# FFN norm statistics from four summed square tiles instead of eight, on eight cores of a Trainium2

## The chip, the cores and the metric

The kernel runs on all 8 cores of one Trainium2 chip, each core with two of the sixteen sequences and no traffic between cores. The metric is the device time of the slowest core in microseconds. The time before is 1403.29 us, the median of 3 runs (1401.22 to 1404.46).

## The reference, cut to what matters

```python
# x: (16, 2048, 1024) f32; weights 1024 x 1024
x = layernorm(x + attn(x))
h = x
for blk in range(3):
    y = qlora_linear(h, q[2*blk], ...)            # dequantised weight + rank-32 term + bias
    y = layernorm(y, gamma[blk], beta[blk])       # over the 1024 features
    y = gelu(y)
    y = qlora_linear(y, q[2*blk+1], ...)
    h = y + h
x = layernorm(x + h)
```

The change is in the inner `layernorm` of the three FFN blocks, in the sum of squares over the 1024 features of a token. The means need no sum: the kernel centres each first weight matrix and its bias over the output features beforehand, so that `y` has mean zero.

## The kernel before, in words

Activations lie transposed: 128 features on the partitions, 512 tokens on the free axis. A sequence has 4 token tiles t of 512, and each of these has 8 feature tiles of 128x512 (`EC = 8`). After attention (which also dequantises the six FFN weights in its background) the FFN runs for each of the core's two sequences g and each block n: `y1(t, n)` for t = 0 to 3, then `y2(t, n, g)` for t = 0 to 3, or in block 2 `y3(t, g)`, which ends with the final norm and the output.

In `y1` each feature tile o is a group: 8 matmuls 128x512 into one PSUM bank, an Identity activation on ScalarE that evacuates the bank to bf16 `FY[t][o]` with the bias (the "evacuation"), and a VectorE multiply `FY*FY` into a bf16 tile `FSQ` (the "square"). A statistic matmul of a matrix of 1/1024 (`ones_b`) with the square adds it into a further bank; after tile 7 this bank holds the variance on all partitions. `finish` (L914) then has ScalarE take Ln and Exp, which gives `FRS`, 1/sqrt(var). VectorE multiplies each `FY` tile by it (L924, the "scaling", bf16 by f32 to bf16), and ScalarE applies Gelu.

The order on every engine's queue is the order in which the Python code emits it. `after_groups(k, fn)` (L195) runs fn at the k-th following `group_end`. A call from inside group o with k = 3 therefore stands behind two further groups on TensorE: the statistic of tile o stands behind group o+2. The Ln of one token tile stands behind group 1 of the next one, so a norm and its Gelus run beside the `y1` of the next token tile.

`pre(0.75, 0.75)` at the start of each group and `post()` at its end place the waiting work: for each group 0.75 scalings (and in block 2, 0.75 of the residual splits of `split_res`, VectorE, bf16 from f32) go onto VectorE's queue ahead of the group's square, and the Gelu of that scaling goes onto ScalarE's queue behind the group's evacuation. The pattern is six scalings and six Gelus in eight groups; the ones left over follow in the next token tile. With t = 0 there is no earlier norm of the block to place.

All instructions are recorded by helpers: L217 is every matmul, L221 every activation, L225 every VectorE tensor-tensor operation, L234 every scalar-tensor-tensor operation. `Queue.put` turns tokens into semaphore waits; a token of the same engine is waited for too (`_waits`, L82).

```python
    FRS = [f32v(a, 512) for a in F_RS]
    FSQ = [b16v(F_SQ + s * 256, 512) for s in range(5)]
```

Of the kernel before, what the change touches and what calls it, by code (L numbers as in the profile page):

```python
# [12 lines left out]
ALU = mybir.AluOpType  # L13
# [5 lines left out]
EC = 8  # L19
# [10 lines left out]
A_P2 = 26624  # L30
# [6 lines left out]
A_MU = 49408  # L37
A_RS = 49920
# [8 lines left out]
F_HB = (0, 6144, A_H + 4096, A_V + 4096)  # L47
F_Y = (A_DO, A_R0, A_H + 6144, A_V + 6144)
F_W = (A_BT, A_WV)
F_RS = (A_P2, A_P2 + 512, A_LORA, A_LORA + 512)  # L50
F_SQ = A_P2 + 1024
F_XR = A_R
F_OUT = (A_R + 2048, A_R + 3072, A_R + 4096, A_R + 5120)

# [72 lines left out]
def build_program():  # L127
# [19 lines left out]
    with ExitStack() as ctx:  # L147
# [47 lines left out]
        def after_groups(n, fn):  # L195
            due.append((groups[0] + n, fn))
            due.sort(key=lambda d: d[0])
# [18 lines left out]
        def mm(out, lhsT, rhs, start, stop, *after, sig=False):  # L216
            return pe.put(lambda e: e.matmul(out, lhsT, rhs, start=start, stop=stop),  # L217
                          *after, sig=sig)
# [5 lines left out]
        def v_tt(out, a, b, op, *after):  # L224
            return dve.put(lambda e: e.tensor_tensor(out, a, b, op), *after)  # L225
# [517 lines left out]
        FY = [[b16v(F_Y[t] + c * 256, 512) for c in range(EC)] for t in range(4)]  # L743
        FW = [[b16v(F_W[s] + c * 512, 1024) for c in range(EC)] for s in range(2)]
        FRS = [f32v(a, 512) for a in F_RS]
        FSQ = [b16v(F_SQ + s * 256, 512) for s in range(5)]
        FXR = [f32v(F_XR + s * 512, 512) for s in range(4)]
        FOUT = [f32v(a, 1024) for a in F_OUT]
        s_fh = [slot() for _ in range(4)]
# [119 lines left out]
        fy_free[0] = (do_free[0], do_free[1], p_att)  # L869
        fy_free[1] = (rg_free[0], p_att)  # L870
        fy_free[2], fy_free[3] = (p_att,), (p_att,)
        frs_free = [(p_att,)] * 4
        fsq_free = [p_att] * 5
        act_att = (act.sem, act.n)
        cnt = {"sq": 0, "rs": 0, "xr": 0, "out": 0, "fo": 0}
        finals = []
# [21 lines left out]
        def y1(t, n):  # L898
# [2 lines left out]
            sb = [None]  # L901
            k_g[t] = [None] * EC

            def stat_mm(o, q, tok):
                if o == 0:
                    sb[0], fr = bank_take()
                else:
                    fr = ()
                p = mm(ps[sb[0]][:], ones_b, FSQ[q], o == 0, o == EC - 1, tok, *fr, sig=True)
                fsq_free[q] = p  # L910
                if o == EC - 1:
                    finish(p)

            def finish(p):  # L914
# [20 lines left out]
            for o in range(EC):  # L935
                pre(0.75, 0.75)
                b, fr = bank_take()
                for c in range(EC):
                    p = mm(ps[b][:], FW[s][c][:, o * 128:(o + 1) * 128], FHB[t][c],
                           c == 0, c == EC - 1, k_fw[w][c], k_hb[t][c],  # L940
                           *(fr if c == 0 else ()), sig=c == EC - 1)
                late = sq_free if (cnt["sq"] == 4) else ()
                ty = a_act(FY[t][o], ps[b][:], AF.Identity, p, k_fb,
                           *(fy_free[t] if o == 0 else ()), *late, bias=fbc(w, o))
                bank_give(b, ty)
                q = cnt["sq"] % 5
                cnt["sq"] += 1
                tq = v_tt(FSQ[q], FY[t][o], FY[t][o], ALU.mult, ty, fsq_free[q])
                post()
                after_groups(3, lambda o=o, q=q, tq=tq: stat_mm(o, q, tq))  # L950
                group_end(8)
            fw_free[s] = (p,)
            fhb_free[t] = (p,)
# [132 lines left out]
        for g in range(NSEQ):  # L1086
            for n in range(NBLK):
                k_res = {t: [None] * EC for t in range(4)} if n == 1 else (k_res if n else {})
                k_lo = {t: [None] * EC for t in range(4)}
                for t in range(4):  # L1090
                    if g == 0 and n == 0:
                        if t == 0:
                            load_h(0, 2)
                            load_h(0, 3)
                        if t in (1, 2):
                            cast_h(t + 1)
                    y1(t, n)
                    if n == 0 and g == 0 and t == 0:

                        while pieces:  # L1100
                            pieces.pop(0)()
                        xr_free = [(rg_free[1],)] * 4
                        fout_free = [(rg_free[2],), (rg_free[2],), (rg_free[3],), (rg_free[3],)]
                    if n == 2:
                        split_res(t)
# [88 lines left out]
```

How the kernel before makes its waits and increments, by code:

```python
    def emit(self, e, last):  # L108
        for todo, fn, sem, by in self.items:
            for s, v in todo:
                e.wait_ge(s, v)
            inst = fn(e)
            if sem is not None:
                inst.then_inc(sem, by)
        for s, v in last:
            e.wait_ge(s, v)
```

## Time and profile before

| what | value |
|---|---|
| median of 3 runs | 1403.29 us |
| the profiled execution, its own time | 1395.1 us |
| its span on the slowest core (core 2) | 1393.5 us |
| spans of the other cores | 1381.3 to 1393.4 us |
| mean granted TensorE clock, by core | 0.975 to 0.981 |

The span runs from the first to the last instruction of the profiled core. The own time is 1.6 us longer, and the median of the unprofiled runs is 8.2 us above it. The FFN takes the part of the span from about 618 us on. In the views, PE is TensorE, DVE is VectorE, ACT is ScalarE, POOL is GpSimd; an "idle before" is the engine's own idle time ahead of an instruction, with what ended it.

### The profile page before, as it was taken

Reading aid. Unit: us, or ns where it says so; the run is one execution under the profiler, and the core shown is the slowest. Engines: PE = TensorE matmul, PEld = TensorE weight load, DVE = VectorE, ACT = ScalarE, POOL = GpSimd, SP = SyncE. Lnnn points to the kernel's source line nnn. Section 1 sums busy time; section 2 is a strip of 40 time slices with the busy share of each in tenths; the row PEclk is TensorE's granted clock in tenths of the full one; section 3 lists DMA queues with packets and bytes.
Section 4 is the critical chain, followed back from the end, with each engine's and each line's share of the span. In section 5 each row is a group of like instructions: output and inputs, shape, how many; then the busy total and the mean of one; then the engine's idle time right before and its main releaser. Section 6 shows DMA issues by size and latency. Waiting matters only on the chain.

```text
span 1393.5 us, 21058 instructions; the slowest of 8 cores (1381.3 to 1393.5 us)
## 1 busy us (share of the span) xinstructions
PE 1300.7 (93%) x6611; PEld 611.1 (44%) x6740; DVE 704.3 (51%) x1487; ACT 746.1 (54%) x1100; POOL 356.1 (26%) x284
## 2 busy tenths in 40 slices
PE   5997999898899999999999999999899999999994
PEld 2444444443344444444444444455444444444552
DVE  1133556543344456446553483677435534736774
ACT  0153226663223276536855884776578558748641
POOL 5022333565543225332000075001100000840010
PEclk9998999999999999999999999999999999999997
DMA  9956546796856345692101055025801010640032
GB/s 136 208 187 208 178 142 165 216 254 234 295 146 212 114 152 186 216 364 87 61 1 61 1 198 165 0 98 206 287 16 61 1 61 20 207 137 1 31 121 91
DMA packets 71371, 192.61 MB, mean 138 GB/s; under 512 B 6032, under 2 KB 16864, under 8 KB 68192
## 3 DMA queue, kind: packets, MB, share of 16 engines
q1 hardware_dynamic: 48352, 133.45, 29.1%
q0 software_dynamic: 22912, 57.81, 15.2%
q8 instruction: 57, 0.93, 0.3%
q14 instruction: 50, 0.41, 0.1%
HBM read 158.85 MB, written 46.15 MB: 147 GB/s over the span
## 4 chain that ended last, share of the span: by engine, by line
PE 72%; DMA 10%; DVE 6%; issue 4%; ACT 4%; POOL 2%; SPq 1%; DVEq 0%; ACTq 0%; POOLq 0%
PE ps L217 72%; ACT POOLT L221 4%; DMA POOLT<-qw_t 3%; DMA POOLT<-xt 2%; DMA x1s<-POOLT 2%; DVE POOLT L225 2%; DVE SM L1032 1%; POOL POOLT L105 1%; DVE SM L234 1%; DMA POOLT<-bv_h 1%; SPq L105 1%; DMA POOLT<-sc_t 1%; DMA POOLT<-lb_h 1%; POOL POOLT L684 1%; DVEq L111 0%
## 5 line engine op out<-in xcount | busy, mean ns | idle before, releaser
L217 PE MATMUL ps<-POOLT 128*128 128x512 bf16 (+3 forms) x5476 | 1225.2, 375 | 37.1 <-DMA POOLT<-wq 11.5
L217 PEld LDWEIGHTS ps<-POOLT 128*128 128x128 bf16 x5600 | 532.9, 98 | 664.5 <-issue 91.7
L221 ACT ACTIVATE POOLT<-ps,SM 128x512 bf16<-128x512 f32 (+4 forms) x396 | 262.2, 682 | 249.3 <-PE ps L217 152.2
L225 DVE TENSOR_TENSOR POOLT<-POOLT 128x512 bf16<-128x512 bf16 (+1 forms) x448 | 256.4, 608 | 209.5 <-ACT POOLT L221 187.0
L221 ACT ACTIVATE POOLT<-POOLT 128x512 bf16<-128x512 f32 (+4 forms) x234 | 175.3, 762 | 225.1 <-DMA POOLT<-qw_t 108.1
L225 DVE TENSOR_TENSOR POOLT<-ps,POOLT 128x512 bf16<-128x512 f32 (+1 forms) x186 | 124.2, 688 | 151.9 <-PE ps L217 126.9
L990 POOL TENSOR_TENSOR POOLT<-POOLT 128x512 f32<-128x512 f32 x64 | 89.6, 1424 | 371.1 <-DMA POOLT<-x1s 361.9
L411 POOL TENSOR_TENSOR POOLT<-POOLT 128x1024 f32<-128x1024 f32 x48 | 112.7, 2348 | 263.1 <-DMA POOLT<-sc_t 169.6
L221 ACT ACTIVATE POOLT<-POOLT,CF 128x512 bf16<-128x512 bf16 x192 | 154.3, 808 | 27.5 <-DVE POOLT L225 26.5
L221 ACT ACTIVATE POOLT<-POOLT,SM 128x512 bf16<-128x512 f32 (+2 forms) x120 | 109.8, 917 | 83.3 <-DVE SM L228 47.8
L234 DVE SCALAR_TENSOR_TENSOR POOLT<-ps,SM,POOLT 128x512 f32<-128x512 f32 x128 | 96.1, 750 | 80.8 <-PE ps L217 80.3
L217 PE MATMUL ps<-POOLT,CB 128*128 128x512 bf16 (+2 forms) x331 | 96.8, 383 | 24.5 <-ACT POOLT L221 13.4
L684 POOL TENSOR_TENSOR POOLT<-POOLT 128x1024 f32<-128x1024 f32 x32 | 75.0, 2362 | 54.7 <-ACT POOLT L221 53.5
L221 ACT ACT_TABLE_LOAD x48 | 61.6, 1283 | 34.8 <-PE ps L217 30.7
L105 POOL DMA_DIRECT2D out<-POOLT x28 | 15.0, 535 | 252.0 <-ACT POOLT L221 252.0
L600 DVE TENSOR_REDUCE SM<-ps 128x1 f32<-128x512 f32 (+3 forms) x80 | 48.9, 611 | 39.7 <-PE ps L217 36.4
L217 PEld LDWEIGHTS ps<-POOLT,CB 128*128 128x128 bf16 (+2 forms) x336 | 25.6, 96 | 66.0 <-issue 45.8
L228 DVE TENSOR_SCALAR POOLT<-ps,SM 128x512 bf16<-128x512 f32 (+1 forms) x36 | 26.9, 755 | 45.8 <-PE ps L217 45.0
L1032 DVE BATCH_NORM_STATS2 SM<-ps 128x6 f32<-128x512 f32 x64 | 43.4, 692 | 10.9 <-PE ps L217 9.0
L217 PEld LDWEIGHTS ps<-CB,POOLT 128*128 128x128 bf16 x512 | 34.4, 99 | 15.4 <-issue 0.6
L217 PE MATMUL ps<-CB,POOLT 128*128 128x128 bf16 x512 | 39.5, 221 | 0.0
L105 POOL DMA_DIRECT2D weffs<-POOLT x48 | 28.6, 597 | 41.8 <-ACT POOLT L221 33.4
(53 smaller groups left out, 250.7 us busy)
## 6 DMA issues: line engine op xcount, KB each, us to landing
POOLT<-qw_t SPq DMA_DIRECT2D x48, 512.0 KB, 4.0
POOLT<-sc_t SPq DMA_DIRECT2D x48, 512.0 KB, 5.5
POOLT<-weffs SPq DMA_DIRECT2D x24, 1024.0 KB, 7.8
POOLT<-xt SPq DMA_DIRECT2D x16, 1024.0 KB, 10.5
x1s<-POOLT POOLq DMA_DIRECT2D x16, 1024.0 KB, 9.2
POOLT<-x1s SPq DMA_DIRECT2D x8, 2048.0 KB, 11.8
POOLT<-x1s SPq DMA_DIRECT2D x64, 256.0 KB, 3.1
out<-POOLT POOLq DMA_DIRECT2D x28, 512.0 KB, 3.8
```

Of the source, the lines that this page charges most:

```text
L105: self.items.append((todo, lambda e: e.dma_start(out=out, in_=in_), slot.sem, 16))
L217: return pe.put(lambda e: e.matmul(out, lhsT, rhs, start=start, stop=stop), *after, sig=sig)
L221: return act.put(lambda e: e.activation(out, in_, func, bias=bias, scale=scale, accum_out=acc), *after)
L225: return dve.put(lambda e: e.tensor_tensor(out, a, b, op), *after)
L228: return dve.put(lambda e: e.tensor_scalar(out, a, s1, s2, op0, op1), *after)
L234: return dve.put(lambda e: e.scalar_tensor_tensor(out, a, s, b, op0, op1, accum_out=acc, reverse1=rev), *after)
L411: dq_ab[s] = pool.put(lambda e: e.tensor_tensor(q, q, f32v(a + 1024, 1024), ALU.mult), t, dq_ld[s][1])
L600: t = dve.put(lambda e, b=b, lo=lo, n=n: e.tensor_reduce(col(ro + n), ps[b][:, lo:512], AX.X, ALU.max, negate=True), p)
L684: ta = pool.put(lambda e: e.tensor_tensor(r3, r3, rb, ALU.mult), t, *k_r)
L990: tr = pool.put(lambda e, h=h, q=q: e.tensor_tensor(h, h, FXR[q], ALU.add), kx, hb[o], th)
L1032: tb.append(dve.put(lambda e, b=b, k2=k2, fo=fo: e.bn_stats(sm[:, fo + 6 * k2:fo + 6 * k2 + 6], ps[b][:]), p, *fin_free[i]))
```

## The change

Each pair of feature tiles now gives one bf16 tile to the statistic: both squares are written in f32 into two work tiles `FTMP`, a third VectorE operation adds them and rounds to bf16, and one statistic matmul takes the sum. A norm has four statistic matmuls in the place of eight. The statistic of a pair is put off by three `group_end` calls from inside its odd group, so it stands behind two further groups. There are six `FSQ` tiles for five, in other places, and three of the four `FRS` tiles move to memory that attention used; the first norm's wait `late` goes, and the tiles' new first waits (for attention's last readers) are set after the first `y1`. No work moves on TensorE but the statistics, and none on ScalarE, GpSimd's or SyncE's queues.

```diff
-F_RS = (A_P2, A_P2 + 512, A_LORA, A_LORA + 512)
-F_SQ = A_P2 + 1024
+F_RS = (A_P2, A_MU, A_RS, A_SQ)
+F_TMP = (A_P2 + 512, A_P2 + 1024)
+F_SQ = tuple(A_P2 + 1536 + 256 * i for i in range(3)) + tuple(A_LORA + 256 * i for i in range(3))
...
-            def stat_mm(o, q, tok):
-                if o == 0:
+            def stat_mm(j, q, tok):
+
+                if j == 0:
                     sb[0], fr = bank_take()
...
-                p = mm(ps[sb[0]][:], ones_b, FSQ[q], o == 0, o == EC - 1, tok, *fr, sig=True)
+                p = mm(ps[sb[0]][:], ones_b, FSQ[q], j == 0, j == 3, tok, *fr, sig=True)
                 fsq_free[q] = p
-                if o == EC - 1:
+                if j == 3:
                     finish(p)
...
-                late = sq_free if (cnt["sq"] == 4) else ()
                 ty = a_act(FY[t][o], ps[b][:], AF.Identity, p, k_fb,
-                           *(fy_free[t] if o == 0 else ()), *late, bias=fbc(w, o))
+                           *(fy_free[t] if o == 0 else ()), bias=fbc(w, o))
                 bank_give(b, ty)
-                q = cnt["sq"] % 5
-                cnt["sq"] += 1
-                tq = v_tt(FSQ[q], FY[t][o], FY[t][o], ALU.mult, ty, fsq_free[q])
+                t2 = v_tt(FTMP[o % 2], FY[t][o], FY[t][o], ALU.mult, ty, ftmp_free[0])
+                if o % 2:
+                    q = cnt["sq"] % NFSQ
+                    cnt["sq"] += 1
+                    tq = v_tt(FSQ[q], FTMP[0], FTMP[1], ALU.add, t2, fsq_free[q])
+                    ftmp_free[0] = tq
+                    after_groups(3, lambda j=o // 2, q=q, tq=tq: stat_mm(j, q, tq))
                 post()
-                after_groups(3, lambda o=o, q=q, tq=tq: stat_mm(o, q, tq))
                 group_end(8)
...
+                        frs_free[1:] = [(*rs_free, *mr_free, *sq_free)] * 3
```

VectorE's queue in `y1` of token tile 2, block 1, of the first sequence. The names are all `POOLT`, the one large memory tile; s3 is ScalarE's semaphore, s1 TensorE's, s2 VectorE's own. Before, from a scaling (no wait) on: the squares of tiles 2 and 3 (one row, x2), a scaling, the square of tile 4, a scaling, the square of tile 5, a scaling, the squares of tiles 6 and 7.

```order
L225 TENSOR_TENSOR POOLT<-POOLT 128x512
L225 TENSOR_TENSOR POOLT<-POOLT 128x512 [waits s3,s1] x2
L225 TENSOR_TENSOR POOLT<-POOLT 128x512
L225 TENSOR_TENSOR POOLT<-POOLT 128x512 [waits s3,s1]
L225 TENSOR_TENSOR POOLT<-POOLT 128x512
L225 TENSOR_TENSOR POOLT<-POOLT 128x512 [waits s3,s1]
L225 TENSOR_TENSOR POOLT<-POOLT 128x512
L225 TENSOR_TENSOR POOLT<-POOLT 128x512 [waits s3,s1] x2
```

The same stretch of the changed kernel, from the square of tile 2 on (the numbers of the lines are one higher): square 2, square 3, their sum (waits s2), a scaling, square 4, a scaling, square 5, sum, a scaling, square 6, square 7, sum.

```order
L226 TENSOR_TENSOR POOLT<-POOLT 128x512 [waits s3,s2]
L226 TENSOR_TENSOR POOLT<-POOLT 128x512 [waits s3]
L226 TENSOR_TENSOR POOLT<-POOLT 128x512 [waits s2,s1]
L226 TENSOR_TENSOR POOLT<-POOLT 128x512
L226 TENSOR_TENSOR POOLT<-POOLT 128x512 [waits s3,s2]
L226 TENSOR_TENSOR POOLT<-POOLT 128x512
L226 TENSOR_TENSOR POOLT<-POOLT 128x512 [waits s3]
L226 TENSOR_TENSOR POOLT<-POOLT 128x512 [waits s2,s1]
L226 TENSOR_TENSOR POOLT<-POOLT 128x512
L226 TENSOR_TENSOR POOLT<-POOLT 128x512 [waits s3,s2]
L226 TENSOR_TENSOR POOLT<-POOLT 128x512 [waits s3]
L226 TENSOR_TENSOR POOLT<-POOLT 128x512 [waits s2,s1]
```

A scaling that stood directly behind the square of an odd tile now stands behind the sum as well, and the sum waits for VectorE's own semaphore.

TensorE's queue at the same place. Before, from the last group ahead of a statistic on: the statistic (`POOLT,CB`, CB holding `ones_b`) stands behind every group of 8 matmuls.

```order
L217 MATMUL ps5<-POOLT 128x512 x7
L217 MATMUL ps0<-POOLT,CB 128x512 [waits s2]
L217 MATMUL ps7<-POOLT 128x512 [waits s3]
L217 MATMUL ps7<-POOLT 128x512 x7
L217 MATMUL ps0<-POOLT,CB 128x512 [waits s2]
L217 MATMUL ps3<-POOLT 128x512 [waits s3]
L217 MATMUL ps3<-POOLT 128x512 x7
L217 MATMUL ps4<-POOLT,CB 128x512 [waits s2,s3]
```

In the changed kernel a statistic stands behind every second group.

```order
L218 MATMUL ps0<-POOLT,CB 128x512 [waits s2]
L218 MATMUL ps3<-POOLT 128x512 [waits s3]
L218 MATMUL ps3<-POOLT 128x512 x7
L218 MATMUL ps1<-POOLT 128x512 [waits s3]
L218 MATMUL ps1<-POOLT 128x512 x7
L218 MATMUL ps4<-POOLT,CB 128x512 [waits s2,s3]
```

The statistic of tiles 2 and 3 comes at the same group as the statistic of tile 3 before, behind group 5; that of the last pair behind group 1 of the next token tile, as before.

## Rows read from the trace of the kernel before

**Rows 1.** The page, busy time of each engine and share of the span

```profile
span 1393.5 us, 21058 instructions; the slowest of 8 cores (1381.3 to 1393.5 us)
...
PE 1300.7 (93%) x6611; PEld 611.1 (44%) x6740; DVE 704.3 (51%) x1487; ACT 746.1 (54%) x1100; POOL 356.1 (26%) x284
```

**Rows 2.** Groups by shape: busy us, mean ns | idle before, releasers

```profile
L225 DVE TENSOR_TENSOR POOLT<-ps,POOLT 128x512 f32<-128x512 f32 x64 | 43.1, 689 | 69.3 <-PE ps L217 59.7 <-DMA POOLT<-xt 9.4
...
L225 DVE TENSOR_TENSOR POOLT<-POOLT 128x512 bf16<-128x512 f32 x64 | 43.8, 685 | 0.0
...
L225 DVE TENSOR_TENSOR SM<-SM 128x2 f32<-128x2 f32 x45 | 7.3, 162 | 5.0 <-DVE SM L234 0.5
...
L217 PE MATMUL ps<-POOLT,CB 128*128 128x512 bf16 x203 | 75.9, 381 | 13.9 <-DVE POOLT L225 10.0 <-ACT POOLT L221 3.7
```

**Rows 3.** Window 1150 to 1200 us: PE, PEld, DVE, ACT, POOL busy; clock; DMA

```profile
1150.00:1200.00 50.00, 48.89 (x224) 22.09 (x227) 29.19 (x49) 43.53 (x60) 10.24 (x7) 1.00 0.27 89
```

**Rows 4.** Timeline of TensorE, statistic matmuls: start, us, what, idle before

```profile
1150.13 1.89 PE L217 MATMUL ps<-POOLT 128*128 128x512 bf16 x8
1151.86 0.38 PE L217 MATMUL ps<-POOLT,CB 128*128 128x512 bf16 x1
...
1160.24 0.38 PE L217 MATMUL ps<-POOLT,CB 128*128 128x512 bf16 x1 [0.45 <-DVE POOLT L225]
...
1176.39 0.38 PE L217 MATMUL ps<-POOLT,CB 128*128 128x512 bf16 x1 [0.45 <-DVE POOLT L225]
```

**Rows 5.** Timeline of ScalarE over the norm between token tiles 1 and 2

```profile
1152.12 0.69 ACT L221 ACTIVATE POOLT<-ps,SM 128x512 bf16<-128x512 f32 x1 [0.56 <-PE ps L217]
1152.70 0.80 ACT L221 ACTIVATE POOLT<-POOLT,CF 128x512 bf16<-128x512 bf16 x1
1153.52 1.28 ACT L221 ACT_TABLE_LOAD   x1
1154.82 0.69 ACT L221 ACTIVATE POOLT<-ps,SM 128x512 f32<-128x512 f32 x1
1155.59 0.63 ACT L221 ACTIVATE POOLT<-POOLT 128x512 f32<-128x512 f32 x1
1156.13 0.67 ACT L221 ACTIVATE POOLT<-ps,SM 128x512 bf16<-128x512 f32 x1
1156.82 1.28 ACT L221 ACT_TABLE_LOAD   x1
1158.11 0.81 ACT L221 ACTIVATE POOLT<-POOLT,CF 128x512 bf16<-128x512 bf16 x1
1158.83 1.24 ACT L221 ACTIVATE POOLT<-ps,SM 128x512 bf16<-128x512 f32 x2
1160.79 0.81 ACT L221 ACTIVATE POOLT<-POOLT,CF 128x512 bf16<-128x512 bf16 x1 [0.72 <-DVE POOLT L225]
1161.51 0.67 ACT L221 ACTIVATE POOLT<-ps,SM 128x512 bf16<-128x512 f32 x1
```

**Rows 6.** Timeline of VectorE: square of tile 3, the scaling behind it

```profile
1159.67 0.42 DVE L225 TENSOR_TENSOR POOLT<-POOLT 128x512 bf16<-128x512 bf16 x1 [2.27 <-ACT POOLT L221]
...
1160.01 0.69 DVE L225 TENSOR_TENSOR POOLT<-POOLT 128x512 bf16<-128x512 bf16 x1
```

**Rows 7.** TensorE idle in block 2, and the clock in two windows behind idle time

```profile
957.74 0.59 PE L217 MATMUL ps<-POOLT 128*128 128x512 bf16 x2 [2.47 <-ACT POOLT L221]
...
1002.39 0.38 PE L217 MATMUL ps<-POOLT,CB 128*128 128x512 bf16 x1 [3.74 <-ACT POOLT L221]
...
1336.73 1.02 PE L217 MATMUL ps<-POOLT 128*128 128x512 bf16 x4 [2.23 <-ACT POOLT L221]
...
1000.00:1008.00 8.00, 5.55 (x18) 2.31 (x20) 1.70 (x4) 4.37 (x7) 1.06 (x2) 0.79 0.93 362
...
1337.00:1340.00 3.00, 2.89 (x16) 1.70 (x16) 2.90 (x6) 3.00 (x6) 1.06 (x2) 0.68 0.37 150
```

**Rows 8.** Timeline of VectorE at the FFN's start, GpSimd multiplying beside it

```profile
630.39 4.79 DVE L225 TENSOR_TENSOR POOLT<-POOLT 128x512 bf16<-128x512 bf16 x1 [0.69 <-ACT POOLT L221]
```

More of the change, by code:

```diff
@@ L745, in build_program @@
         FRS = [f32v(a, 512) for a in F_RS]
-        FSQ = [b16v(F_SQ + s * 256, 512) for s in range(5)]
+        FSQ = [b16v(a, 512) for a in F_SQ]
+        FTMP = [f32v(a, 512) for a in F_TMP]
+        NFSQ = len(FSQ)
         FXR = [f32v(F_XR + s * 512, 512) for s in range(4)]
@@ L871, in build_program @@
         fy_free[2], fy_free[3] = (p_att,), (p_att,)
-        frs_free = [(p_att,)] * 4
-        fsq_free = [p_att] * 5
+        frs_free = [(p_att,), None, None, None]
+        fsq_free = [p_att] * NFSQ
+        ftmp_free = [p_att]
         act_att = (act.sem, act.n)
```

## The prediction

> **What bounds the kernel now.** The page comes first: TensorE is busy for 93% of the span, VectorE and ScalarE for about half [rows 1]. By the page alone a matmul less is time less, and VectorE has room. The window of 50 us inside one FFN block then shows that the mean hides something: TensorE 48.89 of 50, but ScalarE 43.53 [rows 3]. So I read the three engines' timelines around one norm.
>
> TensorE [rows 4]. The eight matmuls of a group take 1151.86 − 1150.13 = 1.73 us, 0.216 each; with its statistic a group takes 1.94. The same statistic, that of tile 3, starts at 1160.24 and 1176.39 in two following token tiles: a period of 16.15 us, where 72 matmuls make 15.54. The missing 0.6 is one wait for VectorE at this statistic. The row of all statistic matmuls [rows 2] has 10.0 us idle for VectorE's sake; token tiles 2 and 3 of the six `y1` stages, 12 norms, have this wait of 0.45.
>
> ScalarE [rows 5] tells why. From the last statistic of the norm (1151.86, call it 0): evacuation of group 1 at 0.26, a Gelu, a table load, Ln, Exp, evacuation 2 only at 4.27, a second table load, a Gelu, evacuation 3 at 6.97. The square of tile 3 starts at 1159.67 [rows 6], 7.81 on this scale, and the statistic at 8.38, where TensorE was ready at 4 x 1.94 = 7.77. So at one place of a norm ScalarE, then VectorE, are the last to be waited for.
>
> **What the change removes.** 96 of 192 statistic matmuls at 0.216: 20.7 us if nothing waits. In the 12 norms that wait, it counts only through what ends last there; the other half, 48, lies in token tiles 0 and 1 and the start of `y2`, where no wait stands: 48 x 0.216 = **−10.4 us**.
>
> **What it adds.** On VectorE 96 sums, and 192 squares with f32 results. A sum reads f32: every tensor-tensor row with an f32 operand has 685 to 689 ns [rows 2], and the scaling, with one f32 input, 0.69 [rows 6]. The square of today, all bf16, takes 0.42 [rows 6]. A bf16-to-f32 square does not occur: it lies between 0.42 and 0.69. I take 0.69, since one f32 operand is enough for it in every row. The Trainium skill (VectorE: DVE Perf Modes, "What auto-detection actually checks") lets two elements a cycle through only where every tensor is 16-bit; by that rule the change loses time, with the fast square it would come out even (below).
>
> The sum waits for VectorE's own semaphore. The small VectorE operations that wait so have 5.0 us idle before 45 of them, 0.11 each [rows 2]. Bounds 0 (with the overlap of 0.09 kept, as square and scaling start 0.34 apart for 0.42 of length [rows 6]) and 0.25; I take 0.11. The skill's same page ("The DRAIN you can't avoid") says a semaphore between two VectorE operations costs nothing extra. By that a link of the chain below shrinks to 3.55 and the total to about 1408; the row has 0.11, and I follow the row.
>
> **Where it lies.** On the new queue a scaling stands behind each odd tile's square and the sum; its Gelu stands on ScalarE ahead of the next evacuation. That closes a chain which TensorE isn't part of. One link: evacuation 3 to square 3, 0.84 (1158.83 to 1159.67 [rows 5, 6]); square and semaphore 0.69 + 0.11; sum, start to start with the scaling behind it, 0.60 (0.69 less the overlap); scaling to Gelu 0.78 (1160.01 to 1160.79 [rows 5, 6]); Gelu to evacuation 5, 0.72 (1160.79 to 1161.51 [rows 5]). Together **3.74 us** for two groups. In the same way from evacuation 5 to 7 and from 7 to 1 of the next token tile. From evacuation 1 to evacuation 3 over both table loads it is 1158.83 − 1152.12 = 6.71 [rows 5], ScalarE's own work, unchanged. A round is 3 x 3.74 + 6.71 = **17.93 us**. TensorE needs 68 matmuls, 14.7 us, and waits for the rest, some 3 us, at the statistic of tiles 2 and 3. Before, the link was 1161.51 − 1158.83 = 2.68 [rows 5], the round 14.75, and TensorE's 16.15 ended last. So each of 12 norms costs 17.93 − 16.15 = 1.78 more: **+21.4 us**.
>
> In block 2 the residual splits share VectorE: for a pair 0.80 + 0.60 for the squares, 0.60 for the sum, 1.5 scalings and 1.5 splits at 0.60 each, 3.80 in all, against TensorE's 17 matmuls, 3.67. In token tile 1 of both passes, where TensorE was the bound, that is 4 x 0.13 each, **+1.0 us**.
>
> The other edits have one answer together, nothing: the places of the tiles, the dropped `late`, and the new first waits, on attention's last readers, which ended long before the second norm. At the FFN's start VectorE operations of 4.79 us stand beside GpSimd's multiplies [rows 8]; four more operations there may cost or move 1 or 2 us; I take 0.
>
> Sum: −10.4 + 21.4 + 1.0 = **+12.0 us**. The profiled execution's span of 1393.5 becomes 1405.5, its own time of 1395.1 becomes 1407.1. The median shown is 8.2 above that execution, so the forecast is 1403.3 + 12.0 = **1415.3 us**. A measurement of this kernel tells about 0.2%, 2.8 us, from no change.
>
> **The clock.** TensorE's idle of 3 us is new. Idle of 2.47 us left the clock at its high level, 2.4 GHz; idle of 2.23 and of 3.74 did not: the granted clock was 0.68 over the 3 us from 1337 and 0.79 over the 8 us from 1000, 1.2 GHz for part of each [rows 7]. The latter is 0.21 x 8 = 1.7 us of matmul time lost. In the new round TensorE has slack of 1.1 between its groups and the chain (statistic at 2.5 behind evacuation 3, then 17 matmuls and 0.26 to evacuation 7: 6.4, against the chain's 7.5), so a fall costs 0.6, or 7 us if all 12 norms have one. That is the top of the forecast's own range, 1408 to 1423. The skill (TensorE: Matmul & The Clock Gate, "What's actually happening") has activity release the throttle and idleness bring it back; no run yet shows which of these waits would.
>
> **The rivals.**
> - *The square stays at 0.42.* Link 3.47, round 17.12: 12 x 0.97 = +11.6, less 10.4: 1404.5 us, no change. For it: nothing but that no row has this operation. Against: all f32 rows.
> - *The chain doesn't close*, since ScalarE makes up its lag between evacuations 3 and 1. Then only the pair's own path is late: evacuation 3 at 6.97 + 0.84 + 0.80 + 0.69 + 0.15 = 9.45, then four groups and two statistics, 7.34: a round of 16.79. 12 x 0.64 − 10.4 = −2.7: 1400.6 us, just at the bound of faster. It decides if the link falls below the 3.67 us that TensorE takes for a pair; mine is above by 0.07 only, but TensorE's start is late too, so it would have to fall a good deal. With 0.42 squares as well it is −5.9, 1397.4.
> - *VectorE's work is hidden, as the page's 51% suggests.* The waits stay at 0.6 and all 96 matmuls count: −20.7, 1382.6 us. This needs the pair's sum ready at 7.34, while evacuation 3 alone starts at 6.97. I see no way.
> - *That the change doesn't do what it says*: the order shows it does.
>
> **Chances.** Forecast 0.66 (with the clock's share); fast square 0.10; open chain 0.17, on both sides of the 0.2% bound; all hidden 0.04; the rest, a size wrong upwards past 1424, 0.03. Faster 0.16, same 0.14, slower 0.70. Range 1400 to 1424 us: from the open chain to the forecast with every clock fall. The likeliest case alone has 1408 to 1423.
>
> **What would show it.** Right: 96 statistic matmuls fewer; two VectorE groups at about 0.69 where the 0.42 squares were; waits of about 3 us on VectorE at the statistic of tiles 2 and 3 in token tiles 2 and 3 of all six stages, 17.9 us apart; ScalarE's Gelus waiting for VectorE after each odd tile. Wrong: waits of 2 us or less there, rounds near 16.8, squares of 0.42, or token tiles 0 and 1 of blocks 0 and 1 longer than 14.7 us. Only the clock would be off if the rounds are longer than 17.9 with a granted clock under 1.00.

## The result and the profile after

The changed kernel takes **1437.8 us** (median of 4 runs, the fastest 1434.9) against 1402.3 before (median of 4); the ratio is 1.0242, 95% interval 1.0222 to 1.0263. So it is slower by 34 us by the ratio, where 12 were forecast and 1424 was the top of the range. A later measurement of the same kernel (e0) gave 1.0253 (1.0201 to 1.0305). Times are medians over all executions, while ratios leave out those in which the cores of one die had a lower granted clock and took some per cent longer.

The page of the changed kernel, the lines that answer to [rows 1]:

```profile
span 1436.7 us, 21083 instructions; the slowest of 8 cores (1415.3 to 1436.7 us)
...
PE 1314.8 (92%) x6644; PEld 605.3 (42%) x6644; DVE 818.9 (57%) x1583; ACT 745.1 (52%) x1100; POOL 355.0 (25%) x284
```

VectorE has 115 us more work and still only 57% of the span. TensorE is busy for 14 us more with 96 matmuls fewer (weight loads x6644 for x6740; some matmul records are missing on the page of before). The groups by shape of core 0, which answer to [rows 2]: line, engine, operation, shapes, count, busy us, mean ns, idle before and its releasers.

```profile
L226 DVE TENSOR_TENSOR POOLT<-POOLT 128x512 bf16<-128x512 bf16 x192 | 139.9, 729 | 0.0
L226 DVE TENSOR_TENSOR POOLT<-POOLT 128x512 f32<-128x512 bf16 x192 | 136.9, 715 | 124.1 <-ACT POOLT L222 123.7
L226 DVE TENSOR_TENSOR POOLT<-POOLT 128x512 bf16<-128x512 f32 x160 | 114.9, 720 | 13.5 <-DVE POOLT L226 8.2 <-PE ps L218 0.2
...
L218 PE MATMUL ps<-POOLT,CB 128*128 128x512 bf16 x110 | 40.9, 383 | 48.8 <-DVE POOLT L226 48.2 <-issue 0.3
```

The second row is the squares, f32 out of bf16; singly they take 0.69 us, and a few that were held up longer raise the mean to 0.715. The third holds the 96 sums and 64 residual splits; 8.2 us of idle there are the sums' waits for VectorE's own semaphore. The last row is the statistic matmuls: they wait for VectorE for 48.2 us, where it was 10.0.

The chain of the forecast can be read off directly. ScalarE on core 0, second sequence, block 1, in the round of token tile 2:

```profile
1180.20 1.24 ACT L222 ACTIVATE POOLT<-ps,SM 128x512 bf16<-128x512 f32 x2
1183.22 0.81 ACT L222 ACTIVATE POOLT<-POOLT,CF 128x512 bf16<-128x512 bf16 x1 [1.78 <-DVE POOLT L226]
1183.94 0.67 ACT L222 ACTIVATE POOLT<-ps,SM 128x512 bf16<-128x512 f32 x1
...
1188.28 0.69 ACT L222 ACTIVATE POOLT<-ps,SM 128x512 bf16<-128x512 f32 x1 [0.51 <-PE ps L218]
...
1198.75 0.67 ACT L222 ACTIVATE POOLT<-ps,SM 128x512 bf16<-128x512 f32 x1
```

VectorE at the same time (square of tile 3, then the sum with three operations behind it, the first of them the scaling):

```profile
1180.97 0.69 DVE L226 TENSOR_TENSOR POOLT<-POOLT 128x512 f32<-128x512 bf16 x1 [1.94 <-ACT POOLT L222]
1181.83 2.50 DVE L226 TENSOR_TENSOR POOLT<-POOLT 128x512 bf16<-128x512 f32 x4 [0.17 <-DVE POOLT L226]
```

Evacuation 3 starts at 1180.20, its square at 1180.97, the sum at 1181.83, the Gelu at 1183.22, evacuation 5 at 1183.94: 3.74 us, the forecast's link to the hundredth. That it is so exact is luck in part: evacuation to square took 0.77 for the 0.84 forecast, square to sum 0.86 for 0.80, and the two misses cancel. TensorE's waits at the statistics of this block:

```profile
1168.49 0.38 PE L218 MATMUL ps<-POOLT,CB 128*128 128x512 bf16 x1 [0.38 <-DVE POOLT L226]
1182.67 0.38 PE L218 MATMUL ps<-POOLT,CB 128*128 128x512 bf16 x1 [2.77 <-DVE POOLT L226]
1201.22 0.38 PE L218 MATMUL ps<-POOLT,CB 128*128 128x512 bf16 x1 [2.03 <-DVE POOLT L226]
```

The window behind the middle one: its length, the busy time (and instructions) of PE, PEld, DVE, ACT and POOL, the granted clock and the DMA's share and rate:

```profile
1182.00:1188.00 6.00, 5.33 (x17) 2.15 (x18) 5.01 (x8) 3.59 (x5) 0.00 (x0) 0.72 0.00 0
```

From 1182.67 to 1201.22 are 18.55 us, not 17.93. The clock stood at 0.72 over 6 us: 0.28 x 6 = 1.7 us of matmul time gone. Evacuation 7 came at 1188.28 for TensorE's sake, 0.60 behind the chain (1183.94 + 3.74 = 1187.68). This is the forecast's "a fall costs 0.6", and it happened.

The FFN's start holds the largest single wait. TensorE, then VectorE, then GpSimd in the timeline of core 7:

```profile
638.89 0.59 PE L218 MATMUL ps<-POOLT,CB 128*128 128x512 bf16 x1 [8.56 <-DVE POOLT L226]
...
627.34 13.60 DVE L226 TENSOR_TENSOR POOLT<-POOLT 128x512 f32<-128x512 bf16 x6
...
627.31 5.08 POOL L685 TENSOR_TENSOR POOLT<-POOLT 128x1024 f32<-128x1024 f32 x2 [12.81 <-ACT POOLT L222]
632.93 0.59 POOL L106 DMA_DIRECT2D x1s<-POOLT  x1 [0.54 <-POOL POOLT L685]
633.54 4.64 POOL L685 TENSOR_TENSOR POOLT<-POOLT 128x1024 f32<-128x1024 f32 x2
```

Six VectorE operations, worth 4 us, lie over 13.6 us. Three of them run beside GpSimd's four multiplies; seen singly they are two squares and their sum:

```profile
627.34 2.85 DVE L226 TENSOR_TENSOR POOLT<-POOLT 128x512 f32<-128x512 bf16 x1
630.12 2.82 DVE L226 TENSOR_TENSOR POOLT<-POOLT 128x512 f32<-128x512 bf16 x1
633.04 5.70 DVE L226 TENSOR_TENSOR POOLT<-POOLT 128x512 bf16<-128x512 f32 x1
```

The sum ends at 638.74, and the statistic that waits for it starts at 638.89. The other three operations come behind the last multiply and take 0.69 or less each. Before, the longest wait at this place was 1.77 us (core 2).

**A measure for the experiments.** Runs differ by some us, also in attention's part. So below stands "the FFN": from the start of VectorE's first 128x2048 cast to the end of the span, as the median of the eight cores. Within a kernel the cores agree here to 1 or 2 us. It is 778.7 us before and 811.3 for the changed kernel in e0, +32.6; the two cores of the changed kernel's first run that had no spells of a clock of 0.81 (see e0) have 810.5 and 811.1. So it is compared across measurements too, e0 being the reference. A "round" is from one norm's Ln to the next; a "tail" from the last Ln of a block's `y1` over its `y2` or `y3` to the next block's first Ln. In blocks 0 and 1 before (past the first block's start): rounds of 16.24, 16.15, 16.35 and a tail of 69.9. A round so measured is that of ScalarE's Lns: the round of token tile 1 in the changed kernel is 16.99 by the Lns (1159.19 to 1176.18 on core 0) and 15.30 by TensorE's last statistics (1156.93 to 1172.23).

### The profile page after: what moved, and what is told of

It reads as the page before. It is cut to its first block, busy times and chain, and to the rows that moved or that the text cites. A ratio compares the mean times of both kernels' runs of the same rounds, so it can differ in the third digit from the quotient of the medians.

```text
span 1436.7 us, 21083 instructions; the slowest of 8 cores (1415.3 to 1436.7 us)
## 1 busy us (share of the span) xinstructions
PE 1314.8 (92%) x6644; PEld 605.3 (42%) x6644; DVE 818.9 (57%) x1583; ACT 745.1 (52%) x1100; POOL 355.0 (25%) x284
## 4 chain that ended last, share of the span: by engine, by line
PE 56%; DVE 11%; DMA 10%; issue 9%; ACT 9%; POOL 2%; SPq 1%; DVEq 1%; ACTq 0%; POOLq 0%
PE ps L218 56%; ACT POOLT L222 7%; DVE POOLT L226 7%; DMA POOLT<-qw_t 4%; DMA x1s<-POOLT 3%; DMA POOLT<-xt 2%; ACT L222 2%; DVE SM L1039 1%; POOL POOLT L106 1%; DVE SM L235 1%; DMA POOLT<-bv_h 1%; SPq L106 1%; DVEq L112 1%; POOL POOLT L685 0%; DMA POOLT<-sc_t 0%
## 5 line engine op out<-in xcount | busy, mean ns | idle before, releaser
L218 PE MATMUL ps<-POOLT 128*128 128x512 bf16 (+2 forms) x5600 | 1242.7, 380 | 26.7 <-ACT POOLT L222 9.2
L226 DVE TENSOR_TENSOR POOLT<-POOLT 128x512 f32<-128x512 bf16 (+2 forms) x544 | 373.2, 721 | 137.7 <-ACT POOLT L222 123.8
L218 PE MATMUL ps<-POOLT,CB 128*128 128x512 bf16 (+2 forms) x240 | 63.7, 387 | 64.1 <-DVE POOLT L226 50.1
L218 PEld LDWEIGHTS ps<-POOLT,CB 128*128 128x128 bf16 (+2 forms) x240 | 16.1, 95 | 104.8 <-issue 98.6
L1039 DVE BATCH_NORM_STATS2 SM<-ps 128x6 f32<-128x512 f32 x64 | 43.2, 689 | 8.0 <-PE ps L218 6.1
L235 DVE SCALAR_TENSOR_TENSOR POOLT<-POOLT,ps 128x512 f32<-128x512 f32 x48 | 30.9, 681 | 14.6 <-POOL POOLT L412 12.3
```

The source lines that it names most:

```text
L235: return dve.put(lambda e: e.scalar_tensor_tensor(out, a, s, b, op0, op1, accum_out=acc, reverse1=rev), *after)
L1039: tb.append(dve.put(lambda e, b=b, k2=k2, fo=fo: e.bn_stats(sm[:, fo + 6 * k2:fo + 6 * k2 + 6], ps[b][:]), p, *fin_free[i]))
```

## The experiments

Theories at the outset: the **chain** (as in the forecast, with too little allowed for the clock and the start) and, as rival, **VectorE's amount of work**, with the order of no account. Diffs are against the changed kernel unless another is named. Ratios are to the kernel before on the same chip.

**e1, the statistic one group later.**

```diff
-                    after_groups(3, lambda j=o // 2, q=q, tq=tq: stat_mm(j, q, tq))
+                    after_groups(4, lambda j=o // 2, q=q, tq=tq: stat_mm(j, q, tq))
```

> The changed kernel, each pair's statistic one group later (three groups behind the pair's odd tile instead of two). Chain theory (the round evacuation, square, sum, scaling, Gelu, next evacuation, with Ln and Exp at its end, and TensorE waiting for the sum of tiles 2 and 3): the wait of 2.8 us at that statistic falls under 1.5 in token tiles 2 and 3, their rounds come down from 17.9 to 15.4 to 17, and the time to 1410 to 1422 us. Rival, VectorE's amount of work is the bound: the rounds stay at 17.9 and the time within 5 us of 1437.8.

Measured: 1417.9 us, ratio 1.0171 (1.0149 to 1.0193), the FFN 798.7, rounds of 18.0, 17.05, 17.4, just above the 15.4 to 17 worked out. The amount of work is the same and 12.6 us are gone, so VectorE's work alone isn't the bound in blocks 0 and 1. In block 2 the rounds grew, to 19.2, 18.8, 19.3, and the whole block took 147.0 us for e0's 146.3: there it didn't help.

**e2, the sum behind the next scaling.** The sum of a pair isn't issued in its group, but in the next `pre`, behind the scaling.

```diff
+            while sum_q:
+                sum_q.pop(0)()
             credit[1] = min(credit[1] + res_rate, 1.75)
...
-                    tq = v_tt(FSQ[q], FTMP[0], FTMP[1], ALU.add, t2, fsq_free[q])
-                    ftmp_free[0] = tq
+                    def pair_sum(q=q, t2=t2):
+                        ftmp_free[0] = v_tt(FSQ[q], FTMP[0], FTMP[1], ALU.add, t2, fsq_free[q])
+                        k_sum[q] = ftmp_free[0]
+                    sum_q.append(pair_sum)
...
```

> The changed kernel with the sum of a pair put behind the next group's scaling on VectorE, so that a scaling is never behind a sum. Same operations, same statistic places. Chain theory: the link is 0.6 to 0.8 us shorter, the pair's own path 0.6 longer; rounds about 17.2 instead of 17.9, the time about 5 to 8 us less, 1430 to 1433. Rival, VectorE's amount of work: no change, 1437.8.

Measured: 1421.3 us, ratio 1.0201 (1.0171 to 1.0230), the FFN 802.8, 8.5 less. Rounds 16.3, 17.13, 17.5. The second round was worked out as 17.2. The order counts.

The same run shows what the sum's own wait costs. Square, scaling and sum of core 0 in one row, the sum third:

```profile
791.34 1.90 DVE L226 TENSOR_TENSOR POOLT<-POOLT 128x512 f32<-128x512 bf16 x3 [1.94 <-ACT POOLT L222]
```

Three operations of 0.69 in 1.90 us, each 0.60 behind the one ahead. The sum still waits for VectorE's semaphore, but one operation stands between it and the square that sets it, and nothing is lost. Directly behind the square, as in the change, it starts 0.79 or 0.86 after it.

**e3, both**, e1's place and e2's order; the matmul takes the token of a sum that is issued later.

```diff
-                    after_groups(3, lambda j=o // 2, q=q, tq=tq: stat_mm(j, q, tq))
...
+                    sum_q.append(pair_sum)
+                    after_groups(4, lambda j=o // 2, q=q: stat_mm(j, q, k_sum[q]))
```

> Both: the sum behind the next scaling, and the statistic one group later. Chain theory: nothing closes; rounds 14.7 to 15.3 in blocks 0 and 1, no wait over 0.6 us at a statistic in token tiles 2 and 3 there, hence no fall of the clock there either; time 1395 to 1405 (the FFN's start still costs 7 to 10). Rival, VectorE's amount of work: rounds 17.9, over 1430.

Measured: 1418.0 us, ratio 1.0173 (1.0151 to 1.0195). This ratio says little: in the profiled run cores 0 and 1 had their clock at 0.81 for 161 us, an FFN of 803 to 805, and set the time. The two other executions that the ratio is taken over have such a pair too, cores 2 and 3 or 4 and 5, with a mean clock of 0.951 to 0.953 and some 20 us longer; the slowest of the six other cores took 1391.2 to 1394.6 us in the three. In the profiled run the FFN of the six others is 777 to 783, as before the change, with rounds of 16.0, 15.8, 16.6 and tails of 67.4 in blocks 0 and 1. These rounds were worked out as 14.7 to 15.3; they missed that by a microsecond. Rounds of 17.4 to 18.9 in block 2 and the start, 31.4 to 34.1 for 24.6, took back what blocks 0 and 1 gave.

**e4, the very first token tile as before** (bf16 squares, eight statistics); all others with pairs.

```diff
+            old = first_y1[0]
...
+                if old:
...
+                    tq = v_tt(FSQ[q], FY[t][o], FY[t][o], ALU.mult, ty, fsq_free[q])
+                    after_groups(3, lambda j=o, q=q, tq=tq: stat_mm(j, q, tq))
...
```

> The changed kernel, with the very first token tile of the FFN as before (bf16 squares, eight statistic matmuls), where GpSimd's multiplies run beside it. Theory, a VectorE operation with two SBUF tensors is held until GpSimd's multiply ends, and the changed kernel has six such operations ahead of its first waiting statistic instead of fewer: the wait of 8.6 us falls to 2 to 4 and the time to 1428 to 1432. Rival, the longer start comes from attention's end or from the moved tiles: the wait stays over 7 us and the time within 3 us of 1437.8.

Measured: 1422.3 us, ratio 1.0197 (1.0179 to 1.0216), the FFN 803.3, 8.0 less. From the first cast to the first Ln it is 24.6 us on six cores (25.9 and 26.0 on two), to the tenth what it was before; the changed kernel has 31.7 to 34.4.

**e11, attention's last four multiplies on VectorE.**

```diff
+                    if (seq, ic) == (1, 3):
+                        for c in (2 * i, 2 * i + 1):
+                            rc = RG[g][:, c * 512:(c + 1) * 512]
+                            ta = v_tt(rc, rc, RS, ALU.mult, t, *k_r)
+                    else:
...
```

> The changed kernel with attention's last four multiplies of 128x1024 on VectorE (as eight of 128x512 in f32, some 5 us of work) instead of GpSimd, nothing else. Theory, VectorE operations with two SBUF tensors are held until GpSimd's running multiply ends: VectorE has more to do, yet the wait at the first statistics falls from 8.6 to under 5 us, no VectorE tensor-tensor operation there takes more than 0.7 us, and the stretch from the FFN's first cast to the first Ln falls from 31.7 to 25-29 us. Rival, only VectorE's amount of work counts there: the wait and the stretch get longer.

Measured: one run, 1420.6 us, beside 1397.7 before; the FFN 802.0, 9.3 less, and 21.5 us to the first Ln. VectorE and TensorE on core 6:

```profile
627.24 7.17 DVE L226 TENSOR_TENSOR POOLT<-POOLT 128x512 f32<-128x512 bf16 x11
634.79 3.90 DVE L226 TENSOR_TENSOR POOLT<-POOLT 128x512 f32<-128x512 bf16 x6 [0.37 <-ACT POOLT L222]
...
643.22 0.38 PE L218 MATMUL ps<-POOLT,CB 128*128 128x512 bf16 x1 [1.97 <-DVE POOLT L226]
```

Seventeen operations in 11 us, where six took 13.6 beside GpSimd. With more work on VectorE the time to the first Ln is shorter than before the change (24.6); at the second Ln the two are level, 43.2 us from the first cast and 43.0 before, where e0 has 51.1. VectorE was held by GpSimd's running multiplies; the rival falls.

**e0, the changed kernel again**, with no edit, beside variants.

> The changed kernel itself once more, beside the variants. If the rounds' length (chain, start of the FFN, falls of the clock to half) is all, its ratio to the kernel before is 1.023 to 1.025 here too, and the FFN of a core without stretches at 13/16 of the clock takes 810 us against 778. If stretches at 13/16 made a good part of the first measurement, the ratio is 1.021 or less on a chip that shows none.

Measured: 1429.0 us, ratio 1.0253 (1.0201 to 1.0305), the FFN 809.7 to 811.5 on all cores, none at 0.81 of the clock. In the first measurement six of eight cores had such spells in the FFN, as core 2 here (the clock of this window is 0.83):

```profile
835.00:845.00 10.00, 10.00 (x41) 4.18 (x40) 8.72 (x10) 8.11 (x13) 10.00 (x7) 0.83 0.66 168
```

The spells come in pairs of neighbouring cores, at the same times in both of a pair. Their FFN took 816 to 823 us, that of the two cores without them 810.5 and 811.1. They are no part of the 34 us: in e0's profiled execution there are none, and the ratio is the same. One other of e0's executions (1441.9 us) has a mean clock of 0.949 and 0.952 on cores 6 and 7; without it the ratio of the means is 1.023.

**e5, bf16 work tiles**, so that square and sum are bf16 throughout.

```diff
-        FTMP = [f32v(a, 512) for a in F_TMP]
+        FTMP = [b16v(a, 512) for a in F_TMP]
```

> The changed kernel with bf16 work tiles, so that squares and sums read and write bf16 alone: 0.42 us each instead of 0.69. Everything else, the order too, as in the change. Chain theory: link 3.74 - 0.27 - 0.26 = 3.21 us, rounds about 16.3 instead of 17.9 (TensorE then ends them at the one wait), one wait of about 1.6 us a round, 20 us less than the changed kernel in blocks 0 to 2 together: ratio to before 1.003 to 1.012. Rival, order and waits alone, not the length: ratio over 1.018.

Measured: ratio 1.0015 (0.9982 to 1.0048). The median over all twelve executions, 1404.5 us, misleads; the seven that the ratio is taken over have 1395.3. The FFN is 777.2: 34 us less. The waits on core 3, with the distance worked out beforehand (802.77 − 786.44 = 16.33):

```profile
786.44 0.38 PE L218 MATMUL ps<-POOLT,CB 128*128 128x512 bf16 x1 [1.70 <-DVE POOLT L226]
802.77 0.38 PE L218 MATMUL ps<-POOLT,CB 128*128 128x512 bf16 x1 [1.50 <-DVE POOLT L226]
```

The total fell by more than the 20 us expected, since waits of 1.7 and 1.5 us no longer bring the clock down (two to four low stretches a core in the FFN instead of seven to nine), the start is 26.6 to 28.2 in place of 31.6 to 34.3, and block 2 came back to 139.3 us (the three rounds and the tail, median of the cores) from 146.3; before it took 141.2. The clock and the start were left out of that expectation once more.

**e6, the kernel before, its statistics one group later.**

```diff
-                after_groups(3, lambda o=o, q=q, tq=tq: stat_mm(o, q, tq))
+                after_groups(4, lambda o=o, q=q, tq=tq: stat_mm(o, q, tq))
```

> The kernel before with each statistic one group later, eight of them, bf16 squares. The wait of 0.6 us in 12 norms goes, nothing else changes: 5 to 8 us faster than before, ratio 0.994 to 0.997. If the last wait only moves to the next square, no change.

Measured: 1384.9 us, ratio 0.9915 (0.9890 to 0.9941), the FFN 765.7, 13 less; rounds 16.24, 15.54, 15.7. So one number in the kernel before gives 12 us without any pairs. It is more than expected: the rounds of blocks 0 and 1 give 0.6 each as foreseen, but the two blocks 2 gave 3.7 and 3.3 us, which wasn't foreseen; it came in the tail of the first, 89.1 us for 92.95.

**e7, each of the 96 statistic matmuls twice.**

```diff
-                p = mm(ps[sb[0]][:], ones_b, FSQ[q], j == 0, j == 3, tok, *fr, sig=True)
+                mm(ps[sb[0]][:], ones_b, FSQ[q], j == 0, False, tok, *fr)
+                p = mm(ps[sb[0]][:], ones_b, FSQ[q], False, j == 3, sig=True)
```

> The changed kernel with each of its 96 statistic matmuls issued twice into the same sum (the variance comes out doubled: this part of the computation is changed, for its time alone). By the term of 10.4 us for 48 removed matmuls that stood where nothing waits: here 48 come back there, and the FFN takes about 10 us more than the changed kernel's 810 to 811; the rounds of token tiles 2 and 3 stay at 17.9 to 18.6, since TensorE waits in them anyway. Rival, a statistic matmul costs the same everywhere: 21 us more.

Measured: one run, 1434.1 us, the FFN 816.0: 5 more, neither 10 nor 21. The rounds are 17.0 (unchanged), 17.9 to 18.9 and 18.6; the tails went from 67.7 to 68.7. In blocks 0 and 1 a statistic matmul counts in the tail, with the last pair and token tile 0, and hardly elsewhere. That of token tile 1 doesn't count, though TensorE waits little there (0.38 us in the rows of core 0 above): what it gives is taken back by the wait of token tile 2, which ends when the chain ends.

**e10, pairs in token tiles 0 and 1 only**; the rest of the diff is e4's.

```diff
+            old = first_y1[0] or t >= 2
```

> Pairs only where the working says nothing waits: token tiles 0 and 1 of each block, except the very first tile of the FFN; token tiles 2 and 3 as before. 44 statistic matmuls fewer (9.5 us), the rounds of token tiles 2 and 3 at 16.2: the FFN takes 768 to 772 us against 778, the ratio to before is 0.993 to 0.996. If the slower squares of token tile 1 hand their lag on to tile 2, no gain: 0.998 or more.

Measured: 1398.8 us, ratio 0.9997 (0.9977 to 1.0017), the FFN 781.9, 3 more. First round 17.0 for 16.24, tail 69.1 for 69.9: in blocks 0 and 1 they cancel. The 3 us are block 2's, 142.9 for 141.2 in the first and 137.4 for 136.3 in the second. So the pairs in token tiles 0 and 1 gain nothing. It was the last clause of the expectation that came true, and the same as in e7.

**e8, block 2 as before**; the rest of the diff is e4's.

```diff
+            old = n == 2
```

> The changed kernel with block 2 alone as before (bf16 squares, eight statistics), where the residual splits share VectorE. Of the FFN's 32 us the chain alone would give block 2 a third of the blocks' part. If VectorE's amount of work makes block 2 dear, these two of six blocks hold half of it: the FFN falls from 810-811 to 798-801 us. If block 2 costs what the others do, to 804-806.

Measured: one run, 1418.5 us, the FFN 802.0, 9.3 less, between the two expectations. Two blocks of six hold more than a quarter of the loss. The windows over the rounds of the first block 2, changed (core 7) and before (core 2); the third number group is VectorE:

```profile
890.00:945.00 55.00, 49.57 (x219) 21.59 (x218) 43.66 (x70) 38.33 (x52) 0.00 (x0) 0.97 0.00 1
```

```profile
868.00:916.00 48.00, 46.88 (x215) 21.23 (x217) 27.24 (x53) 36.60 (x49) 0.00 (x0) 1.00 0.00 1
```

VectorE went from 27.2 of 48 to 43.7 of 55 us. The first block 2 took 146.3 us in e0, 145.8 in e2 (order), 147.0 in e1 (place), 143.3 in e3 (both) and 139.3 in e5 (length). So the length of the operations counts most here, and order and place together give less than half of what it gives.

**e13, TensorE kept at work in its wait.**

```diff
+                if j == 1 and t >= 2:
+                    fb, ffr = bank_take()
+                    for i in range(12):
+                        pf = mm(ps[fb][:], ones_b, FW[s][i % 8][:, 0:512], True, True, *ffr,
+                                sig=i == 11)
+                    bank_give(fb, pf)
```

> The changed kernel with twelve matmuls into a spare bank (read by nobody) ahead of the waiting statistic of tiles 2 and 3 in token tiles 2 and 3, so that TensorE works through 2.6 us of its wait of 2.8. Theory, the falls of the granted clock to 1.2 GHz behind these waits cost 0.6 us each where a wait follows and the full 1.7 where TensorE is the bound: no fall in any y1 stage past the FFN's start, rounds of 17.9 throughout, and the FFN 4 to 8 us shorter than the changed kernel's 811, at 803 to 807 us, though 144 matmuls (31 us) were added. Rival, the falls cost nothing: 810 to 814 us.

Measured: 1429.6 us, ratio 1.0208 (1.0156 to 1.0260), the FFN 805.8: 144 matmuls more and 5.5 us less. The statistics of tiles 2 and 3 in TensorE's timeline on core 4:

```profile
680.61 0.38 PE L218 MATMUL ps<-POOLT,CB 128*128 128x512 bf16 x1 [0.18 <-DVE POOLT L226]
698.54 0.38 PE L218 MATMUL ps<-POOLT,CB 128*128 128x512 bf16 x1 [0.17 <-DVE POOLT L226]
```

They are 17.93 us apart, the forecast's round. The spans and granted clocks by die, where e0 had a clock of 0.968 for both:

```profile
die 0 (median of its cores): 1419.2 us, clock 0.976
die 1 (median of its cores): 1421.0 us, clock 0.973
```

Five cores have two low stretches in the FFN left, at its start and in `y3`, and three have five, against seven to nine in e0. So the falls cost about 5.5 us (by the ratios of the two measurements, 1.0253 and 1.0208, 0.45% or 6 us, with intervals that overlap). If the added matmuls cost some time themselves, the falls cost more.

**e9, e12, e14, the corrected versions.** e9 is e5, e3 and e4 together:

```diff
-        FTMP = [f32v(a, 512) for a in F_TMP]
+        FTMP = [b16v(a, 512) for a in F_TMP]
...
+            old = first_y1[0]
...
-                    after_groups(3, lambda j=o // 2, q=q, tq=tq: stat_mm(j, q, tq))
...
+                    sum_q.append(pair_sum)
+                    after_groups(4, lambda j=o // 2, q=q: stat_mm(j, q, k_sum[q]))
```

> Four statistics a norm, bf16 work tiles, the sum behind the next scaling, the statistic one group later, the first token tile of the FFN as before. By the same working no statistic waits in any block: rounds of 14.7 us, 92 statistic matmuls fewer (19.9 us) and the 12 waits of 0.6 (7 us) gone: 22 to 28 us faster than before, ratio 0.980 to 0.985. Rival, the summed statistics cannot pay at all: ratio 1.00 or more.

Measured: 1375.1 us, ratio 0.9853 (0.9816 to 0.9889), the FFN 754.3, 24 less than before, as worked out (22 to 28); rounds 15.4, 14.74, 15.5. The second block of the first sequence (core 2), from its first Ln to the next block's:

```profile
752.42:866.38 113.96, 113.43 (x520) 51.67 (x528) 65.33 (x116) 80.98 (x113) 44.58 (x32) 1.00 0.36 111
```

It holds 528 matmuls, by the weight loads, and 528 x 0.216 is 114.0 us: TensorE no longer waits. The same stretch took 118.64 before and 121.2 to 122.7 in e0.

e12 is e9 with the statistic one more group away:

```diff
-                    after_groups(4, lambda j=o // 2, q=q: stat_mm(j, q, k_sum[q]))
+                    after_groups(5, lambda j=o // 2, q=q: stat_mm(j, q, k_sum[q]))
```

> Experiment e9 (bf16 tiles, sum behind the scaling, first tile old) with the statistic five calls behind its pair. If in e9 a statistic still is what TensorE waits for, 2 to 4 us less than e9's FFN of 754 us; if nothing waits for a statistic there any more, the same within 1 us, or 1 to 3 more, since the norm comes a group later.

Measured: 1373.1 us, ratio 0.9802 (0.9743 to 0.9861) beside e14's runs, the FFN 752.8, 1.5 less than e9. Past the first block, blocks 0 and 1 take 113.96 us in both, so no statistic is waited for there any more. The two blocks 2 gained 1.1 and 1.2 us, which suggests that in them a statistic was still waited for.

e14 is e9 with pairs in the very first token tile too, and e11's multiplies on VectorE:

```diff
-            old = first_y1[0]
...
+                    if (seq, ic) == (1, 3):
+                        for c in (2 * i, 2 * i + 1):
+                            rc = RG[g][:, c * 512:(c + 1) * 512]
+                            ta = v_tt(rc, rc, RS, ALU.mult, t, *k_r)
...
```

> Everything that the runs found together: bf16 work tiles, sum behind the next scaling, statistic one group later, and attention's last four multiplies on VectorE, all six stages with pairs. The FFN's start at 21 us or less, the FFN at 749 to 753 us, ratio to before 0.979 to 0.984.

Measured: **1368.8 us**, ratio 0.9777 (0.9726 to 0.9828), the FFN 750.6. It beats both kernels. Its page:

```profile
span 1365.4 us, 21078 instructions; the slowest of 8 cores (1356.2 to 1365.4 us)
...
PE 1289.0 (94%) x6644; PEld 601.1 (44%) x6644; DVE 736.5 (54%) x1591; ACT 742.9 (54%) x1100; POOL 346.2 (25%) x280
```

The start took 23.9 us, not 21 or less as expected: 0.7 less than before only, and more than e11's 21.5. Its first statistics and so its first Ln stand one group, 1.7 us, further back than e11's; at the second Ln it has 41.4 us for e11's 43.2.

## Why the prediction was wrong

The direction and the chain were right; the amount was a third. Four steps failed: the start and the clock stood in the sum at 0, the saving in token tile 1 was credited, and block 2 was priced too low. The parts, with e13 (no falls of the clock in the rounds) on core 3 against core 7 of before:

| part | forecast | measured | from |
|---|---|---|---|
| FFN's start | 0 | +7.2 | 31.8 − 24.6; e4 −8.0, e11 −9.3 |
| four blocks 0 and 1 | +7.3 | +10.1 | 2.5, 2.4, 2.8, 2.4 |
| two blocks 2 | +4.7 | +10.2 | 5.6, 4.6 |
| clock | 0, at most 7 | +5.5 | e0 − e13 |
| sum | +12.0 | +33.0 | |

The sum agrees with the FFN's 32.6. Core 7 of before is one of the four whose first block 2 is shortest, 140.35 us (141.2 by the median of the cores); by the medians the two blocks 2 cost 4.8 each and the sum is 32.4.

- **Prices.** The square at 0.69 and the sum at 0.69 were right. With their length gone (e5) the loss is gone; with their length kept, order and place (e3) take away nearly as much, 30 us of FFN. The Trainium skill (VectorE: DVE Perf Modes, "What auto-detection actually checks") lets two elements a cycle through only where all tensors are 16-bit; the trace agrees, with 0.69 for the f32 result.
- **The sum's own wait**, 0.11, lies at 0.10 or 0.17, counted from the end of the square. (The row of [rows 2] puts only 0.5 of its 5.0 us down to VectorE's semaphore, so 0.11 was no clean reading.) Sum after square is 0.79 or more from start to start, where an operation that doesn't wait follows after 0.60. The Trainium skill (VectorE: DVE Perf Modes, "The DRAIN you can't avoid") has such a semaphore cost nothing extra. The trace disagrees where the operation directly ahead sets it, and agrees where one operation stands between (e2, 0.60).
- **The closed chain**, 3.74 and 17.93, was right to the hundredth for token tile 2 (with the luck named above), as was the wait of about 3 us (2.77 and what surrounds it). So was its cause: e1 and e2 move only order and place. The third round, 18.4 to 18.8 in e13, is longer than 17.93, and the tail gets 2.2 us shorter where 0.86 was credited; the two nearly cancel.
- **"−10.4 us" for 48 matmuls where no wait stands** is the step that failed in blocks 0 and 1. I credited token tile 1 (4 x 0.216 a block). Its round isn't shorter but longer, 17.0 for 16.24, and e7 shows its matmuls to be worth nothing. With 0.86 a block less, 1.83 becomes 2.7, and 2.4 to 2.8 were measured. The prediction had itself named a token tile 1 over 14.7 us in blocks 0 and 1 as a sign of being wrong.
- **"I take 0" for the FFN's start** failed, though [rows 8] held the answer: a VectorE operation of 4.79 us is one that is held by two of GpSimd's. I priced four more operations there at 1 or 2 us. What mattered was that a pair's statistic needs three such operations, not one: 2.85, 2.82 and 5.70 us ahead of a statistic that then waited for 8.56.
- **Block 2, "+1.0"**, was short by 5 (1.7 of it is token tile 1's again). I priced the splits in token tile 1 only and let the chain's 17.93 stand for tiles 2 and 3, and the tail gain what it gains in the other blocks. The tail before took 92.11 on core 7 (93.0 by the median), in the changed kernel 91.8. How much each of VectorE's queued operations holds up there wasn't taken apart, so this part is located, not explained.
- **The clock** was priced rightly at 0.6 a fall and left out of the sum, since [rows 7] had idle of 2.47 without one. In fact the clock fell behind five of the twelve waits on core 0 of the first run (those of 2.76, 2.98, 2.63, 2.77 and 2.56 us; two others of 2.77 left it high), and behind five of twelve on cores 1 and 3 of e0, also behind ones followed by `y2`, where TensorE is the bound: e0 has tails of 68.5 to 68.7 behind such a round, else 67.6 to 67.7.

The rivals: the square wasn't fast, the chain did close. Two of their prices contradict the prediction's own test, by which the chain opens if the link falls below TensorE's 3.67: the fast square has a link of 3.47 and was still given the chain's round of 17.12, and the case without the sum's wait has 3.55. e5, with fast squares and sums, has rounds of 16.33. My range was built from cases that each changed one term. The start, block 2 and the clock were all terms put at or near their lowest value, and they all went the same way.

## What to carry to other kernels

A queue that interleaves two streams, here squares and scalings, has a chain of its own: what is put between an operation and the one that another engine waits for lengthens every link, and two engines busy for 57% and 52% of the span can then set the pace together. Save the matmul only with operations that stay in the fast form, put the sum behind what others wait for, and move its reader one group away; the same idea then goes from +2.4% to −2.2%. Try the cheap part by itself first: of the 28 us of FFN that e14 gains, the kernel before gets 13 from its own statistics one group later (e6). Price a start and an end on their own, and count a new idle time of TensorE twice, once for itself and once for the clock.

## What the hardware showed that was not expected

- VectorE operations on two SBUF tensors start beside a running GpSimd multiply of 128x1024 f32 but don't finish before it: two squares took 2.85 and 2.82 us and a sum 5.70, over four multiplies of 2.3 to 2.8, and the same kind 0.69 without them (e11). Operations with one input in PSUM were not held: in the trace of before (core 2) 37 of 128x512 (bf16 out of f32) started beside a GpSimd operation and took 0.69 at most, as elsewhere.
- A wait for VectorE's own semaphore costs 0.19 to 0.26 us when the operation directly ahead sets it (0.79 or 0.86 for 0.60 from start to start), and nothing with one operation between (e2).
- Idle of 2.77 us ahead of a full load brought the clock to its low level in about half of the cases, idle of 1.5 to 1.7 in e5 did not in those rounds, and matmuls that nobody reads, in the idle time, kept it up (e13).
- The granted clock stood at 0.81 in spells of 5 to 15 us on six cores in the changed kernel's first run, and for 161 us on cores 0 and 1 in e3. Both times the two cores of a neighbouring pair had it at the same moments. What brings it on stays open; e0's profiled execution, with the same matmuls, had none.
